# Weight lots one slot ahead, query squares summed on ScalarE, widening behind the exponentials, in a fused cross-attention and expert kernel

## What is computed

```python
q = rms_norm(layernorm(x) @ Wq, q_norm_w)     # 16 heads of 128
k = rms_norm(ctx @ Wk, k_norm_w)              # 4 heads, each serves 4 query heads
v = ctx @ Wv
probs = softmax(einsum('bqhd,bkhd->bhqk', q, k) * scale)
x = x + einsum('bhqk,bkhd->bqhd', probs, v).reshape(B, S, 2048) @ Wo
h = layernorm(x); rw, sel = top_k(softmax(h @ gate_w.T), 2)
x = x + scatter_add(silu((h@w1.T) * (h@w3.T)) @ w2.T * rw)   # per expert, up to cap tokens
```

## Time and profile before

| | us |
|---|---|
| median of 3 runs (2700.0 to 2703.79) | 2702.87 |
| the profiled execution | 2703.17 |
| its span, first to last instruction | 2701.5 |

### The profile page before, as it was taken

How to read it: one execution, slowest core, us unless ns; L and a number is a source line. 1 busy time by engine, 2 the same in 40 slices (tenths; PEclk the granted TensorE clock), 3 DMA queues, 4 the chain that set the end, 5 groups by cost and what they waited for, 6 DMA issues and landing times. The chain is left out here.

```text
span 2701.5 us, 51516 instructions
## 1 busy us (share of the span) xinstructions
PE 2455.9 (91%) x12889; PEld 1878.1 (70%) x12889; DVE 2079.6 (77%) x5478; ACT 1646.6 (61%) x4789; POOL 1107.4 (41%) x1279
## 2 busy tenths in 40 slices
PE   6799999999999999999999999999999999838885
PEld 3577777777777777777777777777777777625452
DVE  5778888888888888888888888888888888626554
ACT  3666666666666666666666666666666666514442
POOL 1224434333333343433333334343333334247885
PEclk8999999999999999999999999999999999868876
DMA  4655555555555555555555555555555555438997
GB/s 146 150 119 112 116 124 117 118 119 120 121 118 119 111 115 124 117 118 118 120 121 119 118 111 115 124 118 119 117 120 121 118 117 105 94 111 171 183 187 96
DMA packets 768402, 331.20 MB, mean 123 GB/s; under 512 B 694860, under 2 KB 695116, under 8 KB 768336
## 3 DMA queue, kind: packets, MB, share of 16 engines
q1 hardware_dynamic: 743152, 283.41, 47.1%
q0 software_dynamic: 22912, 43.16, 8.9%
q10 hardware_dynamic: 2304, 4.24, 0.5%
HBM read 108.15 MB, written 57.71 MB: 61 GB/s over the span
## 5 line engine op out<-in xcount | busy, mean ns | idle before, releaser
L918 ACT CAST pt_hi<-work 128x512 fp32r<-128x512 f16 x256 | 159.0, 621 | 655.7 <-DMA work<-work 655.7
L904 ACT ACTIVATE work<-pb,small 128x128 f32<-128x128 f32 x1024 | 454.5, 454 | 51.1 <-DVE small L1062 51.1
L800 PE MATMUL pb<-wo_hi,ot_hi 128*128 128x512 f32 x1024 | 420.1, 410 | 41.2 <-DVE ot_lo L998 41.2
L728 PE MATMUL pb<-wq_hi,x_hi 128*128 128x512 f32 x1024 | 403.2, 394 | 18.9 <-DVE wq_lo L1216 13.6
L728 PE MATMUL pb<-wq_lo,x_hi 128*128 128x512 f32 x1024 | 401.7, 392 | 0.0
L728 PE MATMUL pb<-wq_hi,x_lo 128*128 128x512 f32 x1024 | 401.7, 392 | 0.0
L800 PE MATMUL pb<-wo_lo,ot_hi 128*128 128x512 f32 x1024 | 401.5, 392 | 0.0
L800 PE MATMUL pb<-wo_hi,ot_lo 128*128 128x512 f32 x1024 | 401.3, 392 | 0.0
L1326 POOL TENSOR_TENSOR small<-small 128x4 f32<-128x4 f32 x256 | 171.0, 668 | 530.5 <-DVE small L1044 530.5
L1050 DVE SCALAR_TENSOR_TENSOR work<-pb,small,work 128x128 f16<-128x128 f32 x1024 | 286.8, 341 | 53.4 <-ACT work L894 53.4
L894 ACT ACTIVATE work<-pb,small 128x128 f16<-128x128 f32 x1024 | 291.3, 366 | 6.5 <-DMA work<-work 6.5
(11 more groups left out here) (144 smaller groups left out, 5293.9 us busy)
## 6 DMA issues: line engine op xcount, KB each, us to landing
work<-x SPq DMA_DIRECT2D x128, 256.0 KB, 3.4
work<-cT SPq DMA_DIRECT2D x64, 256.0 KB, 2.7
work<-xT SPq DMA_DIRECT2D x64, 256.0 KB, 3.2
out<-work SPq DMA_DIRECT2D x64, 256.0 KB, 4.1
xn_scratch<-work SPq DMA_DIRECT2D x64, 256.0 KB, 2.2
work<-work SPq DMA_TRANSPOSE x640, 3.2
wq_raw<-wq SPq DMA_DIRECT2D x4, 1024.0 KB, 13.8
wo_raw<-wo ACTq DMA_DIRECT2D x4, 1024.0 KB, 8.9
```

The source lines that it names most:

```text
L728: mm = nc.tensor.matmul(bank[:, :], lhs[a][:, c, :], rhs[b_][:, c, :], start=(c == 0 and n == 0), stop=(c == NC - 1 and n == 2))
L800: mm = nc.tensor.matmul(WO_B[:, :], otp[a][:, h, :], wop[b_][:, g * HPG + h, :], start=(g == 0 and h == 0 and n == 0), stop=(g == NG - 1 a ...
L904: ex = nc.scalar.activation(probs[:, cols], S_B[:, cols], ACT.Exp, bias=nmax[:, h:h + 1], scale=esc, accum_out=psums[:, h:h + 1])
L918: nc.scalar.copy(ptp[0][:, :, :], pT16[:, HI, :]).then_inc(pt_hi, 1)
```

## The change

Three things are moved or replaced.

1. Lots. Lot 0 is worked off before the loop. The others follow `SPLIT_FIRST` and `SPLIT_LAST`: lots 1, 2 and 3 at the head of (-1, 1), lot 4 at the head of (-1, 2), lot 5 at the head of (-1, 3), and the lots of Wo at the end of (0, 1), (0, 2), (0, 3) and (1, 0). PE takes the means by `MEANS`, one slot ahead of the queries that need them. The loads of Wo are issued by ACT in (-1, 2) and (-1, 3). DVE's `scale_weights` moves from (-1, 1) to (-1, 2), behind lot 4, and SP's wait for its first step moves from before the loop to the head of (-1, 3).
2. Squares. `square_q` does four activations of 128x128, each with its running sum; DVE `sum_q` and its semaphore are gone.
3. Widening. `widen_p(before)` stands behind `exps(cur)` on ACT and behind `normalise(cur)` on DVE.

```diff
-            FEED = {(-1, 0): (0,), (-1, 1): (1,), (-1, 2): (2, 3), (-1, 3): (4,), (0, 0): (5,),
-                    (0, 2): (6,), (0, 3): (7,), (1, 0): (8,), (1, 1): (9,)}
+            SPLIT_FIRST = {(-1, 1): (1, 2, 3), (-1, 2): (4,), (-1, 3): (5,)}
+            SPLIT_LAST = {(0, 1): (6,), (0, 2): (7,), (0, 3): (8,), (1, 0): (9,)}
+            MEANS = {(-1, 0): (1,), (-1, 1): (3,), (-1, 2): (4,), (-1, 3): (5,)}
...
-                sp.wait_ge(wqk_done, 1)
...
+                        if g == 3 and isinstance(b, int) and b == -1:
+                            sp.wait_ge(wqk_done, 1)
...
-                        for l in lots(b, g):
-                            if LOTS[l][0] == "q":
-                                mean(l)
+                        for l in lots(MEANS, b, g):
+                            mean(l)
...
                 def square_q(b, g):
                     u = 4 * b + g
                     wait(act, q_done, u + 1)
-                    wait(act, q_ss, u)
+                    wait(act, q_m, u)
                     if g == 1:
                         wait(act, k_ss, b + 1)
-                    nc.scalar.activation(SQ_B[:, :], Q_BS[g % 2][:, :], ACT.Square, scale=1.0 / QS).then_inc(q_sqd, 1)
+                    for h in range(HPG):
+                        cols = slice(h * 128, (h + 1) * 128)
+                        sq = nc.scalar.activation(SQ_B[:, cols], Q_BS[g % 2][:, cols], ACT.Square, scale=1.0 / QS,
+                                                  accum_out=q_ssq[:, h:h + 1])
+                    sq.then_inc(q_ss, 1)
...
+                head_of_lot(0)
...
-                        for l in lots(b, g):
+                        for l in lots(SPLIT_FIRST, b, g):
                             head_of_lot(l)
-                        if g < 2 and isinstance(b, int) and b == 0:
-                            load_wo(6 + 2 * g)
-                            load_wo(7 + 2 * g)
+                        if g >= 2 and isinstance(b, int) and b == -1:
+                            load_wo(2 + 2 * g)
+                            load_wo(3 + 2 * g)
                         if live(last[0]):
                             split_o(*last)
-                        if live(before[0]):
-                            widen_p(*before)
...
                             exps(*cur)
+                        if live(before[0]):
+                            widen_p(*before)
...
+                        for l in lots(SPLIT_LAST, b, g):
+                            head_of_lot(l)
...
-                def sum_q(b, g):
-                    u = 4 * b + g
-                    wait(dve, q_sqd, u + 1)
-                    wait(dve, q_m, u)
-                    nc.vector.tensor_reduce(q_ssq, heads(SQ_B), AX.X, ALU.add).then_inc(q_ss, 1)
...
+                rest_of_lot(0)
...
-                        if g == 1 and isinstance(b, int) and b == -1:
+                        for l in lots(SPLIT_FIRST, b, g):
+                            rest_of_lot(l)
+                        if g == 2 and isinstance(b, int) and b == -1:
                             scale_weights()
                             dve.wait_ge(wqk_done, 6)
-                        for l in lots(b, g):
-                            rest_of_lot(l)
...
-                        if live(before[0]):
-                            widen_p(*before)
...
                             normalise(*cur)
+                        if live(before[0]):
+                            widen_p(*before)
...
-                        if live(far[0]):
-                            sum_q(*far)
...
+                        for l in lots(SPLIT_LAST, b, g):
+                            rest_of_lot(l)
```

More of the change, by code:

```diff
@@ L538, in build @@
             v_hi, v_lo = sem("v_hi"), sem("v_lo")
-            q_sqd, q_ss, q_m, q_r, q_hi, q_lo = (sem(n) for n in (
-                "q_squared", "q_sumsq", "q_meansq", "q_rms", "q_hi", "q_lo"))
+            q_ss, q_m, q_r, q_hi, q_lo = (sem(n) for n in (
+                "q_sumsq", "q_meansq", "q_rms", "q_hi", "q_lo"))
             sc_done, mx_done, nm_done, exp_done, rs_done, p_nrm, p_hi, p_lo = (sem(n) for n in (
@@ L557, in build, with lots @@
             LOTS = [("k", 0), ("q", 0), ("v", 0), ("q", 1), ("q", 2), ("q", 3)] + [("o", n) for n in range(NG)]
-            FEED = {(-1, 0): (0,), (-1, 1): (1,), (-1, 2): (2, 3), (-1, 3): (4,), (0, 0): (5,),
-                    (0, 2): (6,), (0, 3): (7,), (1, 0): (8,), (1, 1): (9,)}
-            def lots(b, g):
-                return FEED.get((b, g), ()) if isinstance(b, int) else ()
+            SPLIT_FIRST = {(-1, 1): (1, 2, 3), (-1, 2): (4,), (-1, 3): (5,)}
+            SPLIT_LAST = {(0, 1): (6,), (0, 2): (7,), (0, 3): (8,), (1, 0): (9,)}
+            MEANS = {(-1, 0): (1,), (-1, 1): (3,), (-1, 2): (4,), (-1, 3): (5,)}
+            def lots(table, b, g):
+                return table.get((b, g), ()) if isinstance(b, int) else ()
             def lot_of(l, wq_, wkv_, wo_):
```

## The result

The changed kernel takes 2713.69 us (median of 6 executions, 2710.26 to 2715.45) against 2701.47 us of the kernel before in the same comparison: a ratio of 1.0044, 95% interval 1.0031 to 1.0057. It is slower by 0.44%. The time lies inside the stated range of 2676 to 2736, but on the other side of no change than the likeliest case, 2700. That it lies inside says little: the range is 60 us wide, and the forecast change was 3 us. In the comparisons further down the kernel before had medians of 2700.87, 2695.9 and 2697.5 us, so kernels of different comparisons are set side by side by their ratios.

What follows compares the result with a forecast made beforehand. The prediction took the serial chain ACT to DVE to ACT as the bound, with PE close behind. From 2703.2 us it summed -15 (beginning), +14 (60 trips) and -2 (end) to 2700, with a range of 2676 to 2736.

Steps and rivals of the forecast that it cites:

- The bound: Regular trips: the serial order ACT to DVE to ACT bounds the kernel at 35.56 us a trip; PE follows close behind.
- All four legs: Times between successive starts of `maxima` on DVE in g = 0 to 3: forecast 9.9, 8.3, 9.85 and 7.8 us.
- Widening: Widening behind the exponentials on ACT: takes 2.92 us a trip out of the chain, itself costs about 0.53 us.
- Squares: Four 128x128 squares with sums on ACT, replacing one of 0.51 us: 0.265 us a head, 1.05 for four, range 0.96 to 1.76.
- 4s - 3.96: Forecast change of a regular trip in us, s being the four squares' time; +0.24 at s = 1.05, break-even at 0.99.
- The skill's price: Squares on ACT, estimated from the Trainium skill's page: 0.29 us a head, 1.16 for four; set aside for the rows.
- Lots: Beginning of the kernel: weight lots and Wo loads moved earlier let b = 3 start about 15 us earlier.
- the first M: First start of `maxima` on DVE: at 64.87 before, forecast at about 51, 14 us earlier.
- The end's -2: Last four slots: almost no square there, relief of 2.3 us in g = 0 outweighs the rest: -2 us.
- The relaxed chain: Rival, regular trips: ACT's longer list hidden, only PE's work bounds; saves 1.34 us a trip, 2606 us; chance 0.05.
- the lots do nothing: Rival, beginning: next lot's mean waits for its load or Wo loads delay keys; gains 3, not 15: 2712; chance 0.08.
- Slower by the squares: Rival, ACT's squares dearer: 2727 us at 0.29 a head, about 2871 at the exponential's price; chance 0.22.

Runs made afterwards that it cites:

- pad_in: Changed kernel plus one 128x256 copy on ACT, feeding nothing, in each slot of b = 3 to 61, right behind the squares: 2778.75 us, ratio 1.0303.
- pad_end: Changed kernel plus one 128x256 copy on ACT, feeding nothing, at the end of each slot of b = 3 to 61: 2707.38 us, ratio 1.0041.
- wo_early: Changed kernel with all four loads of Wo issued in (-1, 2): 2705.09 us, ratio 1.0035.
- lots_only: Changed kernel with the squares and the widening put back as in the kernel before: 2691.16 us, ratio 0.9966.
- lots_widen: Changed kernel with the old `square_q` and `sum_q` put back: 2573.87 us, ratio 0.9522.
- squares_late: Changed kernel with `square_q` moved behind split_q on ACT: 2566.97 us, ratio 0.9516.
- wo_late: Changed kernel with the loads of Wo in (0, 0) and (0, 1), as in the kernel before: 2709.42 us, ratio 1.0048.
- late_early: Changed kernel with `square_q` behind split_q on ACT and all loads of Wo in (-1, 2): 2565.37 us, ratio 0.9516.

## Why the prediction was right and wrong

- **The bound.** Right: one serial chain ACT to DVE to ACT, with PE behind it. All four legs came within 0.05 us, but in part by luck. The squares were about 0.08 us a slot dearer than forecast, and other links about 0.04 shorter, mostly the widening, which steps on by 0.50 to 0.53 where 0.53 and 0.55 stood in the sum. That the chain is the bound, `pad_in` and `pad_end` show directly: 0.30 us more a slot on the chain cost 1.17 us a trip, the same 0.30 off the chain cost 0.04.
- **Widening.** Right: -2.92 us for the earlier exponentials and 0.53 in each slot. Alone it took the trip to 33.80, where the chain gave 35.56 - 2.92 + 2 x 0.53 = 33.70. 33.80 is PE's floor as well, so the sum alone would prove little; three of the four legs agree within 0.03 us.
- **Squares.** This is the step that failed, and it failed by its size. I took 1.05 us for the four, 0.265 a head, and measured are 1.12 to 1.14, 0.28 a head. The duration was right (274 ns for 278 to 285). The overlap was not: I let 105 ns of the activation overlap with the reading, as behind the longer L904, and here it is 0.18 to 0.20 us to the reading for a duration of 0.26 to 0.28, an overlap of about 80 ns. By 4s - 3.96 the 0.08 are 0.32 us a trip, or 19 us. The trip lost 0.41 instead of 0.24, 24.7 us in 60 instead of 14, since other links were 0.15 us shorter than I had them. The prediction says that the whole is slower from 0.28 a head on, and that is a slip: by its own sum 60 x (4s - 3.96) reaches 17 us at s = 1.06, or 0.265 a head. That is the very price it took, for four times 0.265 are 1.06 and not 1.05. So it stood on the place where the sign turns. At 0.28 a head its sum gives 2717.
- **The skill's price.** From the page "ScalarE: Activation LUTs" of the Trainium skill (What ACT_TABLE_LOAD costs) I had estimated 0.29 a head and set it aside, since its formula overshoots L887 by 13 ns. Measured is 0.28, between the two. Its duration of 293 ns is too long here (the row has 274), its overlap of 93 ns nearer than mine.
- **Lots.** Right in sign, too large: 10.5 us at b = 3 instead of 15. The first lot of queries was finished about 2 us later (DVE starts on it at 20.23 for 18.23, behind a first mean on PE of 6.18 us, which was 4.77 in the kernel before, where the keys' products ran ahead of it), and the keys' transposition took 6.4 us, above the 4 to 6 that I had allowed. Together they make most of the 4 us by which the first M is late (54.95 for 51). The queries of (0, 3) then ran late and held ACT 2.19 us. What of this is left at b = 3 isn't shown: `wo_early` took 1.8 us off the first M and nothing off that of b = 3. Nor is the term the lots' alone: `lots_only` is 12.0 us earlier there, and `lots_widen` and `squares_late` (172.71 and 172.78) are 3.4 us earlier than the changed kernel, so the squares cost time in the first 12 slots too. The end's -2 is -2.0.
- **The sum.** 4.5 us too much for the lots and 11 too little for the trips make the 15 by which 2700 missed the profiled execution's 2715.45. Nothing of the trip's mechanism was missing. A balance of -15, +14 and -2 had a sign that neither term could carry, and the chance for slower, 0.35, should have been the largest: the bounds of the square reached 0.71 us upwards and 0.09 downwards.
- **The rivals.** The relaxed chain fell; so did "the lots do nothing" (`lots_only`, 0.9966). "Slower by the squares" is what happened, near its mild end.
- **PE's floor.** Not part of the forecast's sum, but wrong: from PE's idle share I took 34.2 us for its own trip and, later, 33.4. Measured is 33.76 to 33.80 in four kernels in which PE is hardly ever idle (busy 1596.5 to 1600.0 of the 1600 us from 400 to 2000).

## What to carry to other kernels

An engine that is 61% busy can have no room for work that is put between two steps that another engine waits for: look for the slot's serial order, write down the step from each start to the next, and put new work where the engine already waits. Here the place of two lines was worth 5.5%. And where a change is made of parts, time them apart: the sum of 0.4% hid a gain of 4.8% and a loss of 5.5%.

## What the runs showed of the hardware

- A sum taken by an activation costs ACT 0.12 us a piece here (0.28 us a head with it, 0.16 without), in addition to the columns; four of them (0.47 us) cost nearly as much as one square of 128x512 (0.51 us).
- PE's idle time understates what waits cost it. Before, PE was idle 1.34 us of a trip, and the trip without waits is 1.8 us shorter (35.57 to 33.76).
- Large loads hold up a DMA transposition beside them. From the issue of the keys' transposition to the scores it took 8.7 us with two 1 MB loads issued 1.7 and 0.2 us before it (`wo_late`), 6.4 in the changed kernel, and 4.9 and 3.7 where the traffic of the loads (some 400 GB/s) ended about 3 and 1 us behind the issue (`late_early`, issued 46.42, and `wo_early`, issued 47.95). The median of the changed kernel's 640 transpositions, issue to landing, is 3.2 us.
